# Four buffers for the weighted parts of layer 0, and one-hots that compare with integer destinations

## The reference, cut to what matters

```
x = layernorm(x + L0(x, src, dst, edge_attr_4, edge_attr_16))
x = layernorm(x + L1(x, node_vec1, edge_attr_16, edge_attr_4, src, dst))

# L0, one edge: xs is 64 scalars of x[src], xv is 32 vectors of x[src]; es, ev are sh
out_s = xs*es @ W_ss + (xv . ev) @ W_vv            # with constant factors
out_v = (xs @ W_sv) ev + (xv @ W_vs) es
messages = concat(out_s, out_v) * sigmoid(edge_scalars @ W_rad.T + b_rad)
agg = segment_sum(messages, dst)

# L1 has the same form: silu and two products make the edge's weights, 384 numbers are summed
```

## Time and profile before

| | |
|---|---|
| time, median of 3 runs | 4432.25 us (4431.15 to 4434.81) |
| the profiled execution, its own time | 4438.86 us |
| its span, first to last instruction | 4437.1 us |
| PE, DVE, ACT, POOL busy | 83%, 85%, 76%, 71% of the span |
| layer 0, first gather to start of the last | 68.3 to 2122.2 us |
| layer 1, the same | 2263.6 to 4319.2 us |

### The profile page before, as it was taken

One profiled execution on the slowest core, in us unless ns is written; L12 is line 12 of the kernel. 1 busy time (PEld: TensorE's weight loads), 2 busy tenths in 40 slices (PEclk: granted clock), 3 DMA queues, 4 the chain that ended last, 5 costly groups with the idle time before them and its releaser, 6 DMA issues.

```text
span 4437.1 us, 82996 instructions
## 1 busy us (share of the span) xinstructions
PE 3687.0 (83%) x16478; PEld 2482.5 (56%) x16479; DVE 3771.2 (85%) x12731; ACT 3388.9 (76%) x10841; POOL 3164.3 (71%) x3275
## 2 busy tenths in 40 slices
PE   6777777777777777777789999999999999999996
PEld 4666666665666666666654544444444444444446
DVE  4988888888888888888569889899898899999895
ACT  3888888888878888888567778777777777777773
POOL 3777777777777777777257777777777777777770
PEclk8555555555555555555789999999999999999998
DMA  8767777676666676776233333333333333333331
GB/s 263 193 193 195 193 195 193 193 195 194 193 192 194 193 194 194 193 194 193 75 93 102 102 102 103 102 102 103 102 103 102 102 103 102 102 103 103 103 97 37
DMA packets 325663, 642.06 MB, mean 145 GB/s; under 512 B 143470, under 2 KB 175147, under 8 KB 325531
## 3 DMA queue, kind: packets, MB, share of 16 engines
q0 software_dynamic: 181616, 557.94, 46.0%
q1 hardware_dynamic: 144016, 83.75, 6.9%
HBM read 620.55 MB, written 20.88 MB: 145 GB/s over the span
## 4 chain that ended last, share of the span: by engine, by line
issue 24%; POOL 20%; DVE 19%; ACT 15%; PE 13%; DMA 5%; DVEq 3%; POOLq 0%; SPq 0%; ACTq 0%
POOL arena L342 13%; ACT work L414 12%; PE ps L870 8%; POOL work L342 7%; DVE onehot L627 4%; DVE work L580 3%; DVE work L615 2%; DMA srcs<-in_srcs 2%; ACT ps L440 1%; DVE work L622 1%; DVEq L688 1%; DVE work L577 1%; DMA arena<-table,srcs 1%; DVEq L643 1%; DVE arena L635 1%
## 5 line engine op out<-in xcount | busy, mean ns | idle before, releaser
L342 POOL DMA_INDIRECT arena<-table,srcs x1616 | 1555.0, 962 | 539.9 <-issue 488.4
L342 POOL DMA_INDIRECT work<-table,srcs x1616 | 1564.3, 968 | 493.8 <-issue 460.2
L414 ACT ACTIVATE work<-work,dst_sh 128x96 f32<-128x96 f32 (+1 forms) x4848 | 1502.8, 396 | 335.2 <-issue 213.3
L414 ACT ACTIVATE work<-arena,dst_sh 128x96 f32<-128x96 f32 (+1 forms) x4848 | 1416.7, 378 | 412.5 <-issue 290.8
L870 PE MATMUL ps<-work,onehot 128*128 128x384 f32 x3616 | 1335.0, 517 | 159.8 <-DVE onehot L627 93.4
L870 PEld LDWEIGHTS ps<-work,onehot 128*128 128x128 f32 x3616 | 682.5, 198 | 735.4 <-issue 272.8
L870 PE MATMUL ps<-arena,onehot 128*128 128x161 f32 x3616 | 1047.1, 468 | 6.0 <-DVE arena L599 5.8
L870 PEld LDWEIGHTS ps<-arena,onehot 128*128 128x128 f32 x3616 | 895.1, 311 | 130.1 <-issue 113.8
L846 PE MATMUL ps<-wrad,escal 17*128 17x160 f32 x3232 | 543.4, 481 | 503.1 <-DVE arena L599 503.0
L627 DVE TENSOR_SCALAR onehot<-iota,dstf 128x128 f32 x3616 | 801.4, 295 | 16.3 <-DVE arena L635 8.1
L846 PEld LDWEIGHTS ps<-wrad,escal 17*128 17x128 f32 x3232 | 393.0, 300 | 651.5 <-issue 370.8
(11 more groups left out here) (123 smaller groups left out, 2109.8 us busy)
## 6 DMA issues: line engine op xcount, KB each, us to landing
escal<-in_escal SPq DMA_DIRECT2D x404, 98.0 KB
arena<-table,srcs POOLq DMA_INDIRECT x1616, 3.5
work<-table,srcs POOLq DMA_INDIRECT x1616
table<-work SPq DMA_DIRECT2D x49, 224.0 KB, 2.5
dst_sh<-in_dst_sh SPq DMA_DIRECT2D x404, 20.0 KB, 2.7
table<-work SPq DMA_DIRECT2D x7, 784.0 KB, 4.2
acc<-in_xd SPq DMA_DIRECT2D x1, 3920.0 KB, 26.0
arena<-in_xd SPq DMA_DIRECT2D x7, 560.0 KB, 6.1
```

The source lines that it names most:

```text
L342: pool.indirect_dma_start(out=rows[:, j, t, :], out_offset=None, in_=table, in_offset=bass.IndirectOffsetOnAxis(ap=srcs[:, b, j, t:t + 1], ...
L414: last = nc.scalar.activation(u[:, t, to:to + c1 - c0], r[:, t, c0:c1], ACT.Copy, scale=dst_sh[:, j, at:at + 1].bitcast(f32))
```

## The change

`DEEP0` goes from 2 to 4, so that each slot has a buffer of weighted parts of its own in layer 0: `weighted0` grows from 3584 to 7168 numbers a partition of `work`, and the wait at L422 is for the messages of s - 4. In both layers the cast of the destinations goes with its tile and its semaphore, and `select` takes its scalar from `dst_sh`, as int32.

```diff
-DEEP0 = 2
+DEEP0 = 4
...
-        dstf = sb("dstf", [P, 2, TPS])
...
-        s_dstf = [sem(f"dst_as_float{l}") for l in range(2)]
...
                 for t in range(TPS):
                     last = nc.vector.tensor_scalar(onehot[:, b, t, :], iota[:, bass.ds(window * P, P)],
-                                                   dstf[:, j % 2, t:t + 1], None, ALU.is_equal)
+                                                   dst_sh[:, j, t:t + 1], None, ALU.is_equal)
...
                     dve.wait_ge(s_dsh[l][j // PAIR], (i + 1) * 16)
-                    nc.vector.tensor_copy(dstf[:, j % 2, :], dst_sh[:, j, 0:TPS]).then_inc(s_dstf[l], 1)
                     dve.wait_ge(s_agg[l], s + 1)
                     dve.wait_ge(s_add[l], s + 1)
                     add_sums(l, FIRST + j % 2, held(waiting)).then_inc(s_add[l], 1)
                     weight_by_one(l, s, i, j)
-                    dve.wait_ge(s_dstf[l], s + 1)
                     select(j, j % 2, window).then_inc(s_oh[l], 1)
```

## The result

The changed kernel takes 4449.3 us in the median of 16 runs (4440.15 to 4465.02), the kernel before 4435.3 (4428.72 to 4450.91, 16 runs). The ratio is 1.0034, with a 95% interval of 1.0023 to 1.0046: slower by some 14 us, more than the 0.2% that a measurement can tell. The forecast was no change, 4421 to 4441.

What follows compares the result with a forecast made beforehand. POOL's list of gathers was taken as the bound in both layers. From the 4432.25 us median, 1.0 us came off at the start and 0 for cast, buffers, int32 scalar and gather length, giving 4431 us, range 4421 to 4441.

Steps and rivals of the forecast that it cites:

- POOL is the bound in both layers, at a pace of its own: Both loops: 1616 gathers of 0.962 or 0.968 us plus a constant 0.305 us gap set the time; other engines follow.
- A cast costs DVE 0.14 us, which turns into free time: DVE's lists in both loops: removing the cast only adds to 0.66 and 0.50 us already free per supertile.
- how POOL's own gathers fare beside DVE: Gathers in both layers: the casts' effect on gather length taken as 0, bounded by 0 and 50 us.
- the 50 us above the median: Gathers in both layers: mean over median, 16 and 15 ns for each of 1616, 50 us in all.
- the casts' share in them: Gather excess in both layers: 2 us by DVE busy time, or 6 of 50 us by the port-lock rule.
- gathers longer by 6 ns in the mean: Rival, POOL's gathers: DVE's shifted list lengthens them, 10 us to 4441, or 19 on both layers to 4450; chance 0.05.
- windows agree on POOL's busy time: Both layers: six and seven windows agree to 0.3 and 0.4 us, suggesting the gather average hangs on no one alignment.
- The rule of the port: SBUF port: two-port copies, casts and tensor-scalar instructions lock GpSimd out of descriptor writes; casts' share 6 of 50 us.
- The two more buffers are worth 0: Layer 0: ACT gets only one supertile ahead, so the fourth buffer never counts; 0, at most 57 us without POOL's cover.
- ACT's wait for L599 would move to L440: Layer 0, ACT: part of its 41.9 us wait for DVE's messages moves from L414 to L440.
- The int32 scalar costs nothing: One-hots in both layers: int32 scalar adds 0, at most 0.12 us each; median stays near 281 ns.
- 1.0 us gained at the start: Start of layer 0: POOL's first wait shrinks 0.33 us and its `srcs` wait about 0.65; bounds 0 and 1.2.

Runs made afterwards that it cites:

- deadcast_b: The changed kernel with a cast that nobody reads put back at its place; 4433.98 us against 4435.15 for the kernel before, ratio 0.9998.
- twocasts: The kernel before with a second, unread cast in front of the first; 4447.71 us against 4442.5, ratio 1.0011.
- onein: The changed kernel with layer 0's second message addition reading one operand from PSUM, sums wrong; 4431.46 us against 4435.54 for the kernel before, one execution each.
- pairs1: The changed kernel with layer 1's two small additions made as one-operand reductions over pairs; 4464.62 us against 4442.5 for the kernel before, ratio 1.0045.
- nocast_b: The changed kernel with two buffers again, so only the cast is removed; 4444.2 us against 4435.15 for the kernel before, ratio 1.0028.

## Why the prediction was wrong

- *POOL is the bound in both layers, at a pace of its own*: right. The loops follow from count, mean and gap of the gathers after as before: 1616 x (0.973 + 0.305) = 2065 us, 2064.4 in the trace.
- *A cast costs DVE 0.14 us, which turns into free time*: right in kind. DVE's busy time fell by 4.8 and 4.5 us in a window of some 49.4 supertiles, 0.09 to 0.10 us each, where 0.14 was expected.
- **The step that failed** is the term on how POOL's own gathers fare beside DVE, taken as 0. It measures +12.8 us in the two profiled executions, and some +9 us over all traces with and without an instruction at the head. The prediction had found the 50 us above the median, and priced the casts' share in them, 2 us or, by the rule cited, 6. Both are prices for what the cast itself holds up: by the count that is nothing (0.0 us under L671 in the trace before). What it did was to move the others. The case stood among the rivals, gathers longer by 6 ns in the mean, with a chance of 0.05; measured are 3 ns in layer 0 and 5 in layer 1. The argument against it, that windows agree on POOL's busy time, was unsound: POOL's busy time in a window of fixed length is the same whatever a gather takes, since a longer gather only means that fewer fit; the count of gathers is what moves, and that by one.
- *The rule of the port*, from the Trainium skill (SBUF — State Buffer, Who interferes with whom), was read too narrowly: I weighed its sentence on two-port instructions and not the one on two SBUF inputs, which covers L595, L612 and L618. The trace agrees for these, with 12.2 and 11.4 us. For the cast, to which I applied the first sentence, it shows nothing: 11 gathers in either layer began under one, and lost 0.0 us.
- *The two more buffers are worth 0*: right (0.9980 to 1.0009). That ACT's wait for L599 would move to L440 is wrong: 40.6 us in 21 places are still put down to it at L412, where 41.9 in 22 places were the earlier trace rows. With four buffers L422 asks for messages of two supertiles earlier still, and yet the waits stay, so it was hardly what ended them before. What did was not found.
- *The int32 scalar costs nothing*: right, 281 ns in the median in both, and `deadcast_b` agrees.
- *1.0 us gained at the start*: not seen. POOL's first wait is 7.2 us (7.3 before), the second 1.6 instead of 1.2. In other traces the first is 6.0 to 8.6 us, so it varies by more than the term.
- *Why the gathers meet more of DVE's instructions without the cast* is shown only as far as this: it takes an instruction at that place, of either kind, to undo it, and the count in layer 1 is 5 to 8 us lower in the four traces with one than in the three without; with two of them (`twocasts`) it is between. That it works by phase alone, at equal length of DVE's list, was not shown; the kernels for it met the other conditions. The layout of the tiles is open as a rival. Nor do the gathers account exactly for a median of 14 us in the runs: single traces without the instruction differ by 7.5 us in layer 0, and the rest is in part the upper kind of times described at the end. No version beat the kernel before clearly; `onein`, which adds other numbers, was under it by 4 us in one execution.

## What to carry to other kernels

When an engine that never waits sets the pace, ask what stretches its instructions, not only what delays their start: compare the mean with the median, then see what runs on the neighbour as the long ones begin. Work taken off a neighbour that is not the bound can cost time, as it can move everything behind it; try an idle instruction in its place before crediting the work itself. And an engine's free time in a busy-time table is not all to be spent: spending 0.24 us of a seeming 0.59 for each supertile (`pairs1`) brought POOL's waits back.

## What the runs showed of the hardware that was not expected

- An indirect gather of 128 rows holds POOL for 946 to 953 ns in the median, whether a row has 448 or 224 numbers. It takes up to 0.23 us more when the 0.41 us addition with two SBUF operands was running as it began, and in the mean some 0.09 us more where a one-hot lengthens it. When the gather began first, neither it nor the addition was longer. Under a product of 0.82 us with one operand in PSUM nothing of the kind is seen.
- Times of one kernel fall in two groups some 15 to 20 us apart (before: 15 of 16 up to 4439.5, one at 4450.9; changed: 11 up to 4451.9, five from 4461.7 to 4465.0). One trace of the upper kind was caught, that of `twocasts` at 4465.08. Of the 26 us by which it exceeds the trace before, 18 are in the norm between the layers, where groups of seven tiles follow each other at 14.2 to 14.6 us and, for three groups, at 20.5. POOL's additions there in the trace before, and then in that of `twocasts`:

```profile
2203.34 2.17 POOL L384 TENSOR_TENSOR acc<-work 128x896 f32<-128x896 f32 x1 [12.66 <-ACT work L485]
...
2217.53 2.17 POOL L384 TENSOR_TENSOR acc<-work 128x896 f32<-128x896 f32 x1 [11.40 <-ACT work L485]
...
2232.10 2.07 POOL L384 TENSOR_TENSOR acc<-work 128x896 f32<-128x896 f32 x1 [11.77 <-ACT work L485]
```

```profile
2210.56 2.08 POOL L385 TENSOR_TENSOR acc<-work 128x896 f32<-128x896 f32 x1 [17.80 <-ACT work L486]
...
2231.05 2.07 POOL L385 TENSOR_TENSOR acc<-work 128x896 f32<-128x896 f32 x1 [17.80 <-ACT work L486]
...
2251.53 2.08 POOL L385 TENSOR_TENSOR acc<-work 128x896 f32<-128x896 f32 x1 [17.80 <-ACT work L486]
```

  Layer 1 began 158.0 us after layer 0's last gather had ended there, 138 to 140 in nine other traces. Whether the change makes the upper kind more frequent is open. It took 5 of 16 executions against 1 of 16, and 3 of 11 of `nocast_b` against 6 of 70 of the four kernels run with it that have an instruction at the head; but beside `pairs1` nine of 24 executions of the kernel before took 4449 us or more. The loss is there without it: the lower kind alone has a median of 4446.9 us against 4435.3, and 4443.9 against 4434.8 for `nocast_b`.
- The same program took 4435 us at one time and 5922 to 6044 at another, one chip giving both 4442.5 and 5928.5. In the long ones POOL is busy for just as long, and ACT, DVE and PE wait for things that the trace puts down to no engine of the kernel, as in the first rows of the waits of the kernel without the cast:

```profile
ACT hid L490 <- remote: 982.1, 139, 15.3
DVE acc L633 <- remote: 861.7, 109, 12.2
```

  The cause was not looked for. The change's effect has the other sign there, 0.9972 where it was 1.0028 for the same kernel.
